# First stage of a small transformer block: both parts of p ahead of z, and the loads of x and of the image values begun by ScalarE

## The reference

```
attention 1 (16 heads of 16, causal):  q, k, v = x @ c_attn_w + b;  one more key and value per sequence from cond
    p = softmax(q k^T / 4 + mask);  y = (p v) @ c_proj_w + b
attention 2 (linear):  q2, k2 = relu(y Wq^T + bq), relu(y Wk^T + bk);  v2 = y Wv^T + bv
    ctx = q2 (k2^T v2) / max(q2 . sum(k2), 1e-6)
    res = ctx + y;  x1 = x + layernorm(res) * gamma + beta
LSTM over the 64 steps, then a feed-forward layer with FP4 rounding of inputs and weights:  out = x1 + ffn(lstm(x1))
```

## Time and profile before

| | us |
|---|---|
| median of 3 runs | 917.55 (912.46 to 919.34) |
| the profiled execution | 920.51 |
| its span | 918.8 |
| first stage | about 25 to 482 |
| second stage | from about 485 |

### The profile page before, as it was taken

The page is one execution under the profiler, slowest core; times in us unless marked ns, Lnnn a source line. Parts: engine busy times, 40 slices in busy tenths (PEclk is TensorE's granted clock), DMA queues, the critical chain, the costliest instruction groups (busy, mean ns, idle before and its releaser), DMA issues.

```text
span 918.8 us, 23189 instructions
## 1 busy us (share of the span) xinstructions
PE 753.5 (82%) x7370; PEld 455.1 (50%) x7370; DVE 710.9 (77%) x1773; ACT 466.2 (51%) x1207; POOL 459.4 (50%) x596
## 2 busy tenths in 40 slices
PE   3336868788888888888767899999999999999965
PEld 2124545455555555555434455555555555555533
DVE  6077777777777777787553889999999999999983
ACT  2054656566777777777453444444444444444420
POOL 1045768877777777778630233333333333333342
PEclk9657878899999999999698999999999999999997
DMA  5865555677777777777501123332323333233333
GB/s 122 167 181 111 101 108 115 108 139 148 149 147 149 146 148 150 148 148 144 98 24 29 26 53 68 69 61 54 65 64 69 61 66 56 62 67 67 66 64 69
DMA packets 263438, 89.30 MB, mean 97 GB/s; under 512 B 233809, under 2 KB 262353, under 8 KB 263380
## 3 DMA queue, kind: packets, MB, share of 16 engines
q1 hardware_dynamic: 263380, 88.51, 48.5%
HBM read 25.45 MB, written 8.47 MB: 37 GB/s over the span
## 4 chain that ended last, share of the span: by engine, by line
DVE 27%; SPq 20%; issue 14%; PE 8%; ACT 4%; POOL 4%; DMA 3%; DVEq 1%; POOLq 0%; ACTq 0%
SPq L568 7%; SPq L541 5%; DVE fc L1511 4%; SPq L578 3%; PE bank L801 3%; DVE ffn_room L1577 3%; DVE prob L167 3%; DVE bank L164 3%; SPq L547 2%; DVE prob L171 2%; POOL xq L738 2%; DVE ffn_room L1569 2%; DVE ig L1513 1%; DVE bank L166 1%; DVE x_value L170 1%
## 5 line engine op out<-in xcount | busy, mean ns | idle before, releaser
L738 POOL TENSOR_TENSOR xq<-x_value,x_scale 128x256 f32<-128x256 f32 x32 | 29.4, 920 | 208.1 <-DVE x_value L171 208.1
L801 PE MATMUL bank<-gu,xqT 128*128 128x512 f16 (+1 forms) x576 | 127.3, 368 | 6.8 <-DMA xqT<-xq_split 6.8
L941 PE MATMUL bank<-wx,x1T 128*64 128x512 f16 x768 | 108.4, 406 | 8.1 <-DMA x1T<-x_split 7.5
L661 POOL TENSOR_TENSOR prob<-prob,row_max 128x520 f32<-128x520 f32 x64 | 73.7, 1152 | 74.7 <-DVE row_max L1393 74.2
L952 PE MATMUL bank<-wh,h 128*64 128x512 f16 x768 | 95.6, 385 | 0.7 <-ACT h L1215 0.7
L801 PEld LDWEIGHTS bank<-gu,xqT 128*128 128x128 f16 x576 | 56.0, 102 | 66.0 <-issue 13.2
L941 PEld LDWEIGHTS bank<-wx,x1T 128*64 128x64 f16 x768 | 73.8, 204 | 26.8 <-issue 8.2
L1030 PE MATMUL bank<-dn,hqT 128*128 128x256 f16 x576 | 70.3, 278 | 7.4 <-DMA hqT<-ffn_room 6.6
L668 POOL TENSOR_TENSOR p<-prob,p 128x512 f16<-128x512 f32 x64 | 71.6, 1119 | 2.2 <-ACT p L1112 2.2
L1030 PEld LDWEIGHTS bank<-dn,hqT 128*128 128x128 f16 x576 | 54.8, 99 | 26.3 <-issue 18.4
L759 POOL TENSOR_TENSOR ffn_room<-prob,h_fine 128x704 f16<-128x704 f32 x32 | 44.5, 1389 | 42.6 <-DVE h_rows L1522 42.6
(11 more groups left out here) (194 smaller groups left out, 1834.9 us busy)
## 6 DMA issues: line engine op xcount, KB each, us to landing
vimg_in<-image_values SPq DMA_DIRECT2D x64, 68.0 KB, 2.6
x_in<-in_x_columns SPq DMA_DIRECT2D x16, 256.0 KB, 3.0
x_res<-in_x SPq DMA_DIRECT2D x16, 256.0 KB, 3.1
x_rows<-x_rows_sb SPq DMA_DIRECT2D x32, 128.0 KB, 1.8
ffn_room<-x_rows SPq DMA_DIRECT2D x64, 64.0 KB, 2.2
out<-ffn_room SPq DMA_DIRECT2D x64, 64.0 KB, 2.0
add_mask<-in_mask_Bx1x1xS_ff SPq DMA_DIRECT2D x2, 512.0 KB, 7.5
qkT<-qk SPq DMA_TRANSPOSE x64, 4.2
```

The source lines that it names most:

```text
L661: pool.tensor_tensor(prob[:, r, :], prob[:, r, :], row_max[:, r, None].to_broadcast([P, 8, KEYS]), ALU.subtract).then_inc(s["shifted"], 1)
L738: pool.tensor_tensor(blocks(xq, D), blocks(fp4_x.value, D), spread(fp4_x.scale, D), ALU.mult).then_inc(s["xq_ready"], 1)
L801: last = pe.matmul(dst, lhs(a, c), rhs(b, c), start=first and c == 0 and a == b, stop=c == C - 1 and (a, b) == parts3[-1], skip_group_chec ...
L941: last = pe.matmul(bank[e][B * h:B * h + B, :], x1T16[m][:, c, :, at], half_cols(wx16, a, c, h), start=False, stop=True, skip_group_check= ...
```

## The change

ScalarE: both parts of p are made ahead of the negated mean and offset or ahead of onT and z: the order is now o_sum, p's first half, negated mean, offset, k and v, exp of the second half, p's second half, onT, z. After y_rows and before yT, ScalarE now begins three kinds of loads that SyncE began before: x_in (every second step), x_res and the image values. x_res is now loaded for one tile at a time, in every step, and a step earlier in the tile's way (t3 instead of t4), with a semaphore for each parity. GpSimd multiplies z with gamma after both low parts of p instead of before them. SyncE keeps the transposes and x1's store; both transposes to pT now come ahead of the transpose of x1.

```
 SyncE, step:
-            if t1 and (t1.loop is not None or t1.b > 0):
-                image_values(t1)
-            if t4 and t4.parity == 0:
-                after(sp, s["xb_ready"], t4.count(back=1))
-                sp.dma_start(x_res[:, :, :], x_pairs[t4.pair()]).then_inc(xres_loaded, 16)
-            if t1 and t1.parity == 0 and (t1.loop is not None or t1.b < NT - 2):
-                sp.wait_ge(s["xT_lo"], t1.count(2))
-                sp.dma_start(x_in[:, :, :], x_cols_pairs[t1.pair() + 1]).then_inc(x_loaded, 16)
...
+            if t2:
+                probs_turn(t2, 0)
+            if t2:
+                probs_turn(t2, 1)
             if t6:
...
-            if t2:
-                probs_turn(t2, 0)
-                probs_turn(t2, 1)

 GpSimd, step:
-            if t5:
-                pool.wait_ge(s["z_ready"], t5.count())
-                pool.tensor_tensor(zg_rows[:, :], z_rows[:, :], gamma_sb[:, :], ALU.mult).then_inc(s["zg_ready"], 1)
             if t2:
                 probs_lo(t2, 0)
                 image_part(t2, 1)
                 probs_lo(t2, 1)
+            if t5:
+                pool.wait_ge(s["z_ready"], t5.count())
+                pool.tensor_tensor(zg_rows[:, :], z_rows[:, :], gamma_sb[:, :], ALU.mult).then_inc(s["zg_ready"], 1)
...
-                pool.wait_ge(xres_loaded, t4.pair_count())
+                pool.wait_ge(xres_loaded[t4.parity], t4.pair_count())

 ScalarE, step, after o_sum:
+            if t2:
+                probs_hi(t2, 0)
+            if t5:
+                (negated mean, offset)
             if t4:
                 (k and v)
+            if t2:
+                exp(t2, 1)
+                probs_hi(t2, 1)
+            if t3:
+                hi(t3, onT16[:, 0, :], bank[0][:, 0:D], "onT_ps", "onT_hi", "y_ps")
             if t5:
                 (z)
...
                 act.activation(y_rows[:, t3.parity, :], bank[6][:, 0:D], ACT.Copy, scale=1.0 / W_P).then_inc(s["y_sb"], 1)
+            if t1 and t1.parity == 0 and (t1.loop is not None or t1.b < NT - 2):
+                act.wait_ge(s["xT_lo"], t1.count(2))
+                act.dma_start(x_in[:, :, :], x_cols_pairs[t1.pair() + 1]).then_inc(x_loaded, 16)
+            if t3:
+                after(act, s["xb_ready"], t3.count(back=2))
+                act.dma_start(x_res[:, t3.parity, :], x_rows_tiles[t3.number()]).then_inc(xres_loaded[t3.parity], 16)
+            if t1:
+                if t1.loop is None and t1.b == 0:
+                    act.wait_ge(s["vimg_stored"], 16)
+                after(act, s["img_part"], t1.count(2, 2, back=2))
+                for b in range(2):
+                    act.dma_start(vimg_in[64 * b:64 * b + 64, t1.parity].rearrange("p h c -> p (h c)"),
+                                  vimg_sides[b][t1.number()].partition_broadcast(S)).then_inc(vimg_loaded, 16)
+            if t3:
                 hi(t3, yT16[:, 0, :], bank[6][:, D:2 * D], "yT_ps", "yT_hi", "kv2_ps")
```

More of the change, by code:

```diff
@@ L211, in program @@
     x_cols_pairs = x_columns.rearrange("(c p) (n r) -> n p c r", p=P, r=2 * P)
-    x_pairs = x.rearrange("b s d -> (b s) d").rearrange("(n j p) d -> n p j d", j=2, p=P)
+    x_rows_tiles = x.rearrange("b s d -> (b s) d").rearrange("(n p) d -> n p d", p=P)
     mask_sides = mask.rearrange("(n e) u v s -> e n (u v s)", e=2)
@@ L348, in program @@
     vimg_loaded = sem("vimg_loaded")
-    xres_loaded = sem("xres_loaded")
+    xres_loaded = [sem(f"xres_loaded{i}") for i in range(2)]
     hqT_in = [sem(f"hqT_in{i}") for i in range(2)]
@@ L541, in probs_turn @@
             sp.dma_start_transpose(pT[:, r, :], p16[:, r].rearrange("p h i k -> p (h i k)")).then_inc(pT_in[e], 16)
[L543 to L548, removed]
-        def step(tiles):
-            t1, t2, _, t4, _, t6 = tiles
-            if t1 and (t1.loop is not None or t1.b > 0):
-                image_values(t1)
-            if t4 and t4.parity == 0:
-                after(sp, s["xb_ready"], t4.count(back=1))
-                sp.dma_start(x_res[:, :, :], x_pairs[t4.pair()]).then_inc(xres_loaded, 16)
-            if t1 and t1.parity == 0 and (t1.loop is not None or t1.b < NT - 2):
-                sp.wait_ge(s["xT_lo"], t1.count(2))
-                sp.dma_start(x_in[:, :, :], x_cols_pairs[t1.pair() + 1]).then_inc(x_loaded, 16)
+        def step(tiles):
+            t1, t2, _, _, _, t6 = tiles
             if t1:
@@ L1146, in step @@
                 act.copy(by_bank(o_sum[:, :, :]), o_part(1, HD)).then_inc(s["o_copied"], 1)
+            if t2:
+                probs_hi(t2, 0)
+            if t5:
+                act.wait_ge(s["mean_ready"], t5.count())
+                act.activation(neg_mean[:, :], mean_var[:, 0:1], ACT.Copy, scale=-1.0).then_inc(s["neg_ready"], 1)
+                act.wait_ge(s["neg_ready"], t5.count())
+                act.wait_ge(s["rstd_ready"], t5.count())
+                act.activation(offset[:, :], neg_mean[:, :], ACT.Copy, scale=rstd[:, 0:1]).then_inc(s["offset_ready"], 1)
             if t4:
@@ L1162, in step @@
                     .then_inc(s["z_ready"], 1)
[L1163 to L1168, removed]
             ffn_hi(t4, "outer")
-            if t2:
-                probs_hi(t2, 1)
             if t1:
```

## The result

The changed kernel takes **970.0 us** (median of four runs, three of them from 968.08 to 971.15 and one, disturbed, at 3795.75), the kernel before 917.44 (912.46 to 919.34): 1.057 times as long, with a 95% interval of 1.053 to 1.062. The forecast was 944 us, between 907 and 960: the direction was right, the size was half of what came.

A forecast was written before the change was run, and what follows sets the result against it. SyncE's queue was taken as the bound, 11.53 us a step; loads on ScalarE would make it 12.28. Looped steps 15, unrolled 8, first step 2 and stage's end 2 gave +27 us on 917.55: 944 us, range 907 to 960.

The forecast's parts named there:

- that cover: SyncE's x1 transpose behind pT, needed only after the stage; if not covered, 3 us at most, once at stage's end.
- x_split follows x1 with a step to spare: Looped steps: claim, beside moving z behind both parts of p, that this order costs nothing in the loop.
- The loads on ScalarE: Loads between y_rows and yT: 2.2 and 2.9 us, 2.55 on average; looped step 12.28 against 11.53 us, +15 us over twenty.
- the break-even of 1.80 us: Looped steps: time from y_rows to yT at which moving the loads to ScalarE neither gains nor loses.
- The loop of 9.73 us: Looped step from yT through exp, p, k and v, PE and back to y_rows: 5.79 + 3.94 us, without y_rows to yT.
- The loop over qkT: Looped steps: qkT's issue, scores, y's transposes and the split behind yT, put at 10.6 us; next in line after SyncE.
- The new order of p: Looped steps: z and its gamma product behind both parts of p, k and v behind the first; claimed to cost nothing.
- Steps 1 to 9: Steps ahead of the loop: first step +2 us, unrolled steps 2 to 9 +8 us from loads delaying yT.
- the 3.0 of the earlier trace: First step: landing time in us assumed for x's load, with which the delay was put between 0 and 5 us.
- The loads free on ScalarE: Faster rival: issues on ScalarE cost nothing, yT 0.91 us behind y_rows, -18 us in the loop, 900 us; chance 0.18.
- The late landing of x_in: Slower rival: x_in lands after 5.2 us and pushes exp, 1.5 us in ten looped and three other pairs, 963 us; chance 0.07.
- The near break-even: Rival: only the issues count, 1.6 and 2.0 us; looped steps stay at 11.53 us, other steps +5 to +9, 924 us; chance 0.20.

The follow-up runs named there:

- the turn alone: Kernel before, with only SyncE's order edited: both transposes to pT ahead of the transpose of x1; 965.6 us, ratio 1.053.
- the two kernels with added products: Eight unused matmuls added on PE ahead of q2's products: in changed kernel with SyncE's x1 transpose first, 942.2 us; in kernel before with only loads moved, 947.4 us.
- the one try: Changed kernel plus 16 unused matmuls of 256 columns on PE ahead of the outer products in every second step; 970.8 us, ratio 1.059.
- the loads alone: Kernel before with only x_in, x_res and image-value loads moved to ScalarE between y_rows and yT; 961.8 us, ratio 1.047.
- x1T first: Changed kernel with SyncE's transpose of x1 put back ahead of the transposes to pT; 958.1 us, in a second timing 951.55 us, ratio 1.041.

## Why the prediction was wrong

**The step that failed** is this: "SyncE's transpose of x1 goes behind pT; it is needed first after the stage. If that cover goes, its landing at the stage's end, once, costs the 3 us of pT's two issues at most." I asked who reads what the transpose writes, x1T, and that is indeed the next stage. I did not ask who waits for the transpose to have read its source. x1's parts have one buffer, so x1's high part of the next tile (L1189) waits for it in every step, and ScalarE, which takes its work in order, keeps x's high part, q's and k's parts, and exp behind it. Shown from both sides: the turn alone costs 48 us on the kernel before, and with a second buffer the same late transpose costs nothing (0.993 with the loads on SyncE), and the changed kernel falls from 970 to 935 us. It was there to be read: in the kernel's code L1189 stands behind a wait for x1T with back=1, and the trace of before shows no such wait, with x1T begun ahead of pT. "x_split follows x1 with a step to spare" was wrong for the same reason. What it cost in the changed kernel is the 3.12 us in front of x1's high part, in one step of two, and what hangs on it, 35 us in all. Part of that wait is a transfer that I had also left at its old length: x1T lands 4.2 us after its issue in the changed kernel (median of the looped steps) and 2.9 in the kernel before.

**PE's clock** was no term of my sum at all, which is a second thing left at nothing without a reason; I had it at 1.00 in the earlier trace rows and kept it there. With the wait for x1T comes a hole of 2.85 us on PE, behind it the granted clock falls, and the products between v and y_rows take 1.7 us more, in one step of two. The low clock costs where such products stand on the path, as the 2.77 us for 1.46 in front of k show, and the two kernels with added products got 9 and 14 us back, not all of it surely by the clock. In the changed kernel itself it was not separated: the one try delayed v. By the table the wait is 2.4 and the clock 1.7 of 4.1 us a pair, but the second vanishes with the first: with two buffers the granted clock is 0.99. "The Trainium skill", page "TensorE: Matmul & The Clock Gate", section "HAM oscillation — how this bites in real kernels", tells of a kernel whose PE, waiting on DMAs, falls back to the lower clock again and again; the trace agrees, with 0.89 in one step and 1.00 in the next, though PE waits here for v and not for a DMA itself.

**The loads on ScalarE**, the body of the forecast, came out near their size. The issues of the two steps take 0.36 to 0.57 us each; y_rows to yT takes 1.90 and 2.68 us where I had 2.2 and 2.9; the break-even of 1.80 us held in both directions (2.29 on average lost; 1.61 and 1.26 at the most gained). The loop of 9.73 us was measured at 9.62 in the short step. (The loop over qkT adds up to 10.5 us from its own rows and not to 10.6, which changes nothing. And that SyncE's rows carry no wait proved nothing: in the timeline after they carry none either, where SyncE idles for 5 us. The chain in the earlier trace rows is what showed it as the bound.) With the wait for x1T taken out the kernel stands at 935 us, in the range and 9 below my number, and the loads' price is 21 us for 27 expected. What I could not know from before is that this size holds only with pT first: the loads alone, and x1T first, were expected 20 to 40 us faster than they are, since I again left out PE's waits for yT's low part and pT and the clock behind them.

**The new order of p** costs nothing, as said, where SyncE is the bound: 914.2 us, 0.6% faster. Once ScalarE is the bound only the place of k and v was tried, and there the difference (896.0 and 898.9 us) is not resolved.

**Steps 1 to 9** cost 4 us, not 10. In the first step x_in lands 7.8 us behind its issue, and ScalarE waits:

```profile
44.83 0.45 ACTq L1171 DMA_DIRECT2D x_in<-in_x_columns  x1
...
52.68 0.40 ACT L1079 CAST xT<-x_in 128x256 f16<-128x256 f32 x1 [5.47 <-DMA x_in<-in_x_columns]
```

That is more than the 3.0 of the earlier trace rows, and yet the first pT is 1.5 us earlier than before. The sum had VectorE's work hide it; what did was not tested. In the unrolled steps yT came 1.60 to 2.54 us behind y_rows, near the forecast (1.85 and 2.5), but the steps passed on 0.6 us each and not 1.0. Which work hid the rest was not tested. The stage's end cost nothing.

**The rivals.** The loads free on ScalarE: ruled out by the issue rows, 0.33 us at the least. (With them falls the 50 ns that the Trainium skill, page "DMA: Bandwidth & Descriptors", section "Anatomy of one DMA — SWDGE (gpsimd) path", gives for a sequencer's dispatch, as a cost of an issue here.) The late landing of x_in had the time nearest to the result, 963, and is not what happened: the wait for x_in is 0.24 us in the row of the short step and 0.65 at the most anywhere behind the first step. A right number from it would have been chance. The near break-even (924): out, as yT comes at 2.29 us and not 1.80.

**What stays open.** How much of the 4.1 us a pair the clock would cost without the wait. What makes x1T land late beside the loads on ScalarE. Why x1T first, and the loads alone, are still at 942 and 947 us with the added products, when the loop that I worked out gives some 930; part is the clock, which is still at 0.97 and 0.96. And whether k and v ahead of p's first part is worth anything.

## What to carry to other kernels

When a DMA is moved later in its queue, look for two kinds of waiters: those that read what it writes, and those that must not overwrite what it reads. A buffer that exists once turns the second kind into a wait in every step, on an engine that may have nothing else to do with the transfer. An issue moved from a queue to a computing engine has a price there, and it is paid or hidden by its place: the four issues cost 2.4% behind y_rows, and the two of them that fit into waits which are there anyway bring 1.3%, both against the same base with every load on SyncE.

## What the runs showed of the hardware

- An issue of a plain load takes ScalarE 0.34 to 0.64 us in the loop of the changed kernel (0.34 to 0.50 for x, 0.48 to 0.64 for one image value), about as long as SyncE in the earlier trace rows (0.40, and 0.60 to 0.65), and what stands behind it in ScalarE's list waits: yT begins 1.90 and 2.68 us behind y_rows.
- More work on PE made two kernels faster, by 9 and 14 us, and their granted clock was higher (0.97 for 0.96, 0.96 for 0.92 between 205 and 440 us). The low clock showed behind waits of PE: in the changed kernel the granted clock was 0.57 from 255 to 259 us, and the wait of 2.85 us had ended at 253.67. With the turn alone it was 0.88 between 205 and 440 us, and no time in which PE stood still there is longer than 1.83 us; the kernel before has such times of up to 1.32 us and a clock of 1.00. What it takes to lower it was not tested.
- The transpose x1T lands 2.8 to 2.9 us (median) after its issue where it stands behind qkT, with the loads on either engine. Behind pT it lands in 2.4 and 2.5 us with every load on SyncE, in 2.9 and 3.2 with the image values begun by ScalarE, and in 4.2 and 4.5 with all loads begun there. SyncE issues it in 1.19 us behind pT and in some 1.6 behind qkT. So neither its place nor its issue time tells how soon it lands; the loads begun beside it go with it.
